# A graph network's first stage: x times the first weights per node, gathered as 96-float rows

## The reference

```
h = concat([x[src], edge_attr])          # 32 + 16 columns
h = relu(h @ w1a + b1a)                  # 96 columns
h = h @ w1b + b1b
s = segment_sum(h, dst); agg = s / max(count(dst), 1)
```

## Time and profile before

| what | us |
|---|---|
| median of 3 runs | 15099.62 (15078.14 to 15099.76) |
| span of the profiled execution | 18914.5 |
| `prepare`, to the next block's first instructions | 0 to 282 |
| quarters 0 and 1, no groups | 282 to 380 |
| first stage, groups | 380 to 7697 |
| node network | 7697 to 7892 |
| propagation | 7892 to 12603 |
| tensor messages | 12603 to 18914.5 |

### The profile page before, as it was taken

How to read it: one execution, slowest core, us unless ns; L and a number is a source line. 1 busy time by engine, 2 the same in 40 slices (tenths; PEclk the granted TensorE clock), 3 DMA queues, 4 the chain that set the end, 5 groups by cost and what they waited for, 6 DMA issues and landing times. The chain is left out here.

```text
span 18914.5 us, 402579 instructions
## 1 busy us (share of the span) xinstructions
PE 14494.5 (77%) x139778; PEld 9671.3 (51%) x139779; DVE 10873.1 (57%) x15415; ACT 5258.0 (28%) x10677; POOL 7506.3 (40%) x8530
## 2 busy tenths in 40 slices
PE   2666666666666666799999999977787778777877
PEld 2555555555555555655555555544444444444444
DVE  6444444444444444455555555557787777777777
ACT  2333333333333333100000000014444444444443
POOL 4444444444444444000000000026676666666765
PEclk8666666666666666699999999989999999999999
DMA  2100010101010010165666566541111111111111
GB/s 72 23 21 22 21 22 20 23 20 23 21 23 21 21 23 21 60 190 187 190 188 190 188 191 190 171 122 27 27 28 28 28 27 28 28 27 27 28 27 27
DMA packets 1143323, 1240.77 MB, mean 66 GB/s; under 512 B 399134, under 2 KB 1111834, under 8 KB 1142394
## 3 DMA queue, kind: packets, MB, share of 16 engines
q1 hardware_dynamic: 932485, 1124.29, 19.8%
q0 software_dynamic: 210496, 113.01, 4.2%
HBM read 1143.04 MB, written 93.60 MB: 65 GB/s over the span
## 5 line engine op out<-in xcount | busy, mean ns | idle before, releaser
L1500 POOL DMA_INDIRECT m_src<-x_after_layer,m_idx x3240 | 3130.8, 966 | 6032.8 <-DMA m_idx<-in_src 4921.4
L180 POOL DMA_INDIRECT l_xin<-in_x,l_idx x3240 | 3095.0, 955 | 4382.1 <-DMA l_idx<-in_src 3211.4
L1232 PE MATMUL p_prod<-a_slot,f_parts 128*32 128x448 fp8e4 x90552 | 4318.4, 353 | 105.4 <-DVEq L1397 50.6
L1232 PEld LDWEIGHTS p_prod<-a_slot,f_parts 128*32 128x32 bf16 x90552 | 2428.9, 97 | 1932.8 <-issue 115.6
L1631 PE MATMUL radial_ps<-radial_w,radial_hidden 128*128 128x384 f32 x6480 | 2598.2, 538 | 719.1 <-DVE m_products L1770 420.0
L581 PE MATMUL a_ps<-hot_hi,hot_lo 128*128 128x196 bf16 x6272 | 1640.4, 303 | 1902.7 <-ACT a_image L680 958.9
L749 DVE TENSOR_TENSOR hot_hi<-window_hi,number_ps 128x1568 bf16<-128x1568 f32 x784 | 1401.2, 1787 | 2895.4 <-PE degree_ps L582 1502.9
L1636 PE MATMUL m_visit_ps<-m_products,m_onehot 128*128 128x288 f32 x8420 | 2445.4, 440 | 561.8 <-DVE m_onehot L1737 261.8
L1636 PEld LDWEIGHTS m_visit_ps<-m_products,m_onehot 128*128 128x128 f32 x8420 | 1669.8, 201 | 1370.3 <-issue 767.9
L1631 PEld LDWEIGHTS radial_ps<-radial_w,radial_hidden 128*128 128x128 f32 x6480 | 1212.8, 202 | 1992.9 <-issue 793.3
L680 ACT ACTIVATE a_image<-a_ps 128x392 fp8e4<-128x392 f32 x3136 | 1478.5, 496 | 2644.6 <-PE a_ps L581 1672.3
(11 more groups left out here) (203 smaller groups left out, 12640.4 us busy)
## 6 DMA issues: line engine op xcount, KB each, us to landing
a_nibbles<-multiplicity_digit SPq DMA_DIRECT2D x1085, 784.0 KB, 4.4
edge_w<-in_edge_weight SPq DMA_DIRECT2D x324, 320.0 KB
multiplicity_digit<-a_packed SPq DMA_DIRECT2D x392, 196.0 KB
l_xin<-in_x,l_idx POOLq DMA_INDIRECT x3240
m_src<-x_after_layer,m_idx POOLq DMA_INDIRECT x3240
xt<-in_edge_attr SPq DMA_DIRECT2D x324, 80.0 KB, 2.2
edge_directions<-rel_unit SPq DMA_DIRECT2D x12, 675.0 KB
m_unit<-edge_directions SPq DMA_DIRECT2D x324, 25.0 KB
```

What stands on the lines that cost most here:

```text
L180: pool.indirect_dma_start(k.xin[m][:, j, :], None, k.io["x"], bass.IndirectOffsetOnAxis(k.idx[m][:, j:j + 1], 0)).then_inc(k.gathered[m], 16)
L1232: mm = nc.tensor.matmul(view(prod[rows, w, :], 0, [[QW, 2], [1, QW]]), source[:, h * HH + j, r * D:(r + 1) * D], slots[h][:, 2 * w:2 * w + ...
L1500: pool.indirect_dma_start(src[m][:, j, :], None, k.x3_d, bass.IndirectOffsetOnAxis(idx[m][:, j:j + 1], 0)).then_inc(gathered[m], 16)
```

## The change

In `prepare`, PE transposes x in 25 quads of four node blocks, multiplies each by a block-diagonal copy of the first 32 rows of `w1a` and adds the bias by a second product (`first_products`); ACT copies the result and stores it to DRAM as `xw_d`, 96 floats a node (`copy_products`). x is loaded at the start. Of the six early gathers one stands between the two rounds of window rows and five behind the second.

In the first stage the gathers fetch 96-float rows of `xw_d`. The attributes are laid out on 80 partitions. Each of a group's two hidden steps is one product of the attributes with a block-diagonal `w1e` and one product of the identity with the gathered rows, both 480 columns wide, summed in PSUM. The transposes and the copies to `xt` are gone. The products of the first visit stand two at a time between single count pairs (`BETWEEN_STEPS`); DVE writes the first one-hot behind a group's first batch, further visits behind its last.

```diff
 def gather_group(k, pool, m):
     for j in range(G):
-        pool.indirect_dma_start(k.xin[m][:, j, :], None, k.io["x"],
+        pool.indirect_dma_start(k.xin[m][:, j, :], None, k.xw_d,
...
-    RC = 270
+    RC = 216
...
+            sp.dma_start(k.x[:], io["x"].rearrange("(b p) f -> p b f", p=P)).then_inc(x_loaded, 16)
+            sp.dma_start(b_quad[:], ...).then_inc(x_loaded, 16)
+            sp.wait_ge(fine_ready, 1)
+            for j in range(4):
+                sp.dma_start(w_quad[j * D:(j + 1) * D, j * DH:(j + 1) * DH], io["L0_gnn_w1a"][0:D, :]).then_inc(x_loaded, 16)
...
+            def copy_products(t):
+                m = t % STAGES
+                if t >= STAGES:
+                    act.wait_ge(first_stored[m], t // STAGES * 16)
+                for j in quads(t):
+                    n = in_quad(j)
+                    act.wait_ge(first_ready, j + 1)
+                    nc.scalar.copy(view(k.xin[m][:], j % 2 * (4 * DH), [[1, n * DH]]), turn_ps[:, 2 + j % 2, 0:n * DH]).then_inc(first_copied, 1)
+                first, end = 8 * t, min(8 * t + 8, NB)
+                act.wait_ge(first_copied, quads(t).stop)
+                act.dma_start(k.xw_d[first * P:end * P, :].rearrange("(b p) c -> p b c", p=P),
+                              k.xin[m][:, 0:end - first, :]).then_inc(first_stored[m], 16)
...
+            def first_products(t):
+                for j in quads(t):
+                    n = in_quad(j)
+                    pe.wait_ge(x_turned_copied, t + 1)
+                    if j >= 2:
+                        pe.wait_ge(first_copied, j - 1)
+                    to = turn_ps[:, 2 + j % 2, 0:n * DH]
+                    nc.tensor.matmul(to, x_turned[0:n * D, t % 2, j % 2 * P:(j % 2 + 1) * P], w_quad[0:n * D, 0:n * DH], start=True, stop=False)
+                    nc.tensor.matmul(to, ones[:], b_quad[0:1, 0:n * DH], start=False, stop=True).then_inc(first_ready, 1)
...
-STEPS_PAIRS = ((4, 4, 4), (4, 2, 2))
+BETWEEN_STEPS = {3: (2, 2, 2, 1, 1, 1, 1, 2), 2: (1, 1, 2, 1, 0, 1, 0, 2)}
...
             def hidden(g, m, b):
-                pe.wait_ge(xt_evac, g + 2)
                 pe.wait_ge(h_evac, g * 2 + (b + 1))
-                for t in range(HT):
-                    mm = nc.tensor.matmul(h_ps[:, t * DH:(t + 1) * DH], xt[:, m % 2, (b * HT + t) * EP:(b * HT + t + 1) * EP], w1a[:],
-                                          start=True, stop=True)
-                mm.then_inc(h_ready, 1)
+                to = h_ps[:, b, 0:HT * DH]
+                nc.tensor.matmul(to, attr[:, m % 2, b * EP:(b + 1) * EP], w1e[:], start=True, stop=False)
+                nc.tensor.matmul(to, k.ident[:], view(xin[m][:], b * (HT * DH), [[1, HT * DH]]), start=False, stop=True).then_inc(h_ready, 1)
...
-            def visits(g, twos, n):
+            def visits(g, twos, n, between):
...
+                one_hot(onehot[n], first).then_inc(onehot_ready, 1)
+                add(dve.snap(count, min_val=0, max_val=NG * NB))
...
+                between()
+                with dve.If(end - first > 1):
```

More of the change, by code:

```diff
@@ L229, in prepare @@
     ident_ready = sem("ident_ready")
+    x_turned_ready, x_turned_copied = sem("x_turned_ready"), sem("x_turned_copied")
+    first_ready, first_copied = sem("node_first_ready"), sem("node_first_copied")
+    STAGES = 2
+    first_stored = [sem(f"node_first_stored{m}") for m in range(STAGES)]
+    quads = lambda t: range(2 * t, min(2 * t + 2, QUADS))
+    in_quad = lambda j: min(4, NB - 4 * j)
+    TURNS = -(-QUADS // 2)
     rel_loaded = [sem(f"rel_loaded{n}") for n in range(2)]
@@ L297, in _ @@
                                         bass.IndirectOffsetOnAxis(at[0][:, g:g + 1], 0)).then_inc(fine_rows, 16)
-            early(2)
+            for m in range(STAGES):
+                await_alone(pool, k.passed_pool, first_stored[m], len(range(m, TURNS, STAGES)) * 16)
+            early(0)
             await_alone(pool, k.passed_pool, key_stored, 32)
@@ L303, in _ @@
                                         bass.IndirectOffsetOnAxis(at[1][:, g:g + 1], 0)).then_inc(key_rows[g // WD], 16)
-            for m in range(3, NX):
+            for m in range(1, NX):
                 early(m)
@@ new lines, in hidden, with product @@
+                nc.tensor.matmul(to, attr[:, m % 2, b * EP:(b + 1) * EP], w1e[:], start=True, stop=False)
+                nc.tensor.matmul(to, k.ident[:], view(xin[m][:], b * (HT * DH), [[1, HT * DH]]), start=False, stop=True).then_inc(h_ready, 1)
+            def product(m, one, tiles):
+                for j in tiles:
+                    mm = nc.tensor.matmul(visit_ps[:, 0:P], hid[m % 2][:, j, :], onehot[one][:, j, :],
+                                          start=(j == 0), stop=(j == G - 1))
+                if G - 1 in tiles:
@@ L624, in visits @@
                     mm.then_inc(product_done, 1)
                     pe.reg_add(count, count, 1)
-            def group(g, twos, m, turn, q, at):
[L629 to L633, removed]
-                first, end = blocks(pe, g)
-                pairs(q, at, run[0])
-                at += run[0]
-                hidden(g, m, 1)
-                pairs(q, at, run[1])
-                at += run[1]
-                if m < NX - 1:
-                    transposes(g + 1, m + 1, turn)
-                visits(g, m, first, end)
-                pairs(q, at, run[2])
-                return at + run[2]
@@ L646, in _, with further_visits @@
-            pe.wait_ge(weights_loaded, 32)
+            def further_visits(m, first, end):
+                with pe.If(end - first > 1):
+                    with pe.Fori(first + 1, end):
+                        v = pe.snap(count, min_val=0, max_val=NG * NB)
+                        pe.wait_ge(onehot_ready, v + 1)
+                        await_alone(pe, k.passed_pe, added, v + 2)
+                        product(m, 2, range(G))
+            def group(g, twos, m, turn, q, at):
+                runs = BETWEEN_STEPS[BATCHES[m]]
+                first, end = blocks(pe, g)
+                for step, count_pairs in enumerate(runs):
+                    pairs(q, at, count_pairs)
+                    at += count_pairs
+                    if step == 0:
+                        pe.wait_ge(loaded[m % 2], twos * 32 + 32)
+                        pe.wait_ge(gathered[m], turn * (16 * G) + 16 * G)
+                    if step < 2:
+                        hidden(g, m, step)
+                    elif step < 7:
+                        tiles = range((step - 2) * 2, (step - 1) * 2)
+                        if step == 2:
+                            v = pe.snap(count, min_val=0, max_val=NG * NB)
+                            await_alone(pe, k.passed_pe, h_evac, g * 2 + 3)
+                            await_alone(pe, k.passed_pe, onehot_ready, v + 1)
+                            await_alone(pe, k.passed_pe, added, v + 2)
+                        if step == 4:
+                            await_alone(pe, k.passed_pe, h_evac, g * 2 + 4)
+                        product(m, m % 2, tiles)
+                further_visits(m, first, end)
+                return at
@@ L647, in _ @@
+            pe.wait_ge(weights_loaded, 16 * HT)
             pe.wait_ge(zero_ready, 1)
```

142 lines of the change are left out of this document (73 added, 69 removed).

## The result

The changed kernel takes 15156.02 us (median of 4 runs, 15137.57 to 15180.15), the kernel before 15097.29 (15078.14 to 15099.76): a ratio of 1.0045, 95% interval 1.003 to 1.0059, so 45 to 89 us more. Forecast were 15,131 and 31 us more.

What follows compares the result with a forecast made beforehand. The prediction took POOL's ten gathers a group to bound the first stage. Wider gathers, PE's work and the shorter chain counted 0, prepare +31 us: 15099.6 + 31 = 15,131, range 14,860 to 15,320.

Steps and rivals of the forecast that it cites:

- The reading of the first stage: First stage: POOL's ten gathers a group set its pace, to within 283 us.
- The late signals: First stage, profiled: PE's signals arrive after POOL's gathers have ended; the profile's own, 3814.9 us over the unprofiled time.
- the floor of 3930 and the cap of 4213: First stage, unprofiled: at least POOL's gathers plus issue time, 3930 us; at most what other stages leave, 4213 us.
- the shorter chain from gather to relu: First stage, transposes and copies gone: taken as 0, lower end -283 us, since SP loads indices six groups ahead.
- its 283 us: First stage: the gap between its least and greatest unprofiled length, where any waits at handoffs had to be.
- point 3 of prepare: Prepare: ACT's 13 turns end at 90 us (half clock 118), seven direction pieces at 126, under 132.
- the half-clock end (+53): Prepare: upper end of its growth, +53 us, if PE's products ran at half clock and direction pieces ended at 154.
- The other terms of prepare: Prepare: window numbers some 8 us later, second round 147.5 to 213.2, 50 gathers 62.6 us, POOL through at 275.8.
- The first rival: First stage waited at handoffs, not at POOL's pace: up to 283 us gained, 14,848 with prepare; chance 0.36.
- My sum of PE's records: First stage: PE gets 0.45 us a group more at full clock, up to 1.35; costed at nothing beside POOL.
- The second rival: First stage bound by PE at a mean clock of 0.757: 190 us slower, 15,320 with prepare; chance 0.12.
- The third: Prepare: its growth is hidden because the window-part chain ends it at 275 in either kernel, about 15,100; chance 0.10.

Runs made afterwards that it cites:

- The first experiment: On the changed kernel, seven of ACT's square roots stand between the node products' turns instead of behind all 13: 15129.92 us, ratio 1.0034.

## Why the prediction was right in direction, and 28 us short

**The reading of the first stage held.** The late signals were the profile's own, and the old stage, seen without them, is at POOL's pace: 4114 us, between the floor of 3930 and the cap of 4213. Two terms made the floor 184 too low, some 90 us each. The mean gather of the earlier trace rows is 952 ns, and without late signals it is 980, because in the old trace only 9 gathers of the loop were held up by a packing, not 54. The issue time of 872.6 us is 962.4 there, because in the old trace some 300 gathers (an estimate: 90 us at 0.30 each) stood behind a wait instead. The ten gathers a group are still there, at the same price for wider rows, so the stage is as long as before (4121 against 4114).

**Luck has a part in that.** The prediction put the shorter chain from gather to relu at nothing, because SP loads indices six groups ahead. What the runs show is a near tie: with half of the gathers the old stage still takes 4100 us, 14 less than with all. Had the other engines needed some 100 us more, the same edit would by these rows have shortened the stage, and the prediction could not tell: it had only its 283 us.

**The step that failed is point 3 of prepare**, the end of ACT's turns. I took 90 us (118 at half clock) and saw the direction pieces covered by the first round of window rows. Each product of 384 columns takes 1.64 us for its two records (0.79 from start to start), where the sum had 0.355 a record from the earlier trace rows. ACT's turns end at 123.8, the seventh piece at 162, and the second round starts at 177.58 instead of 147.5. The first experiment gives that back in the trace (27.4 us). So the first end of the sum was right in its mechanism, "to 154, and then 22 us are late", and the choice was wrong: I took the messages' full-clock row, and PE ran the node products at the half clock. Their records have the durations of that level (ns min/median/max; the products, then records of 384 columns in the messages from 9504.7 to 9509.7 us at a granted clock of 0.50, and from 9548.9 to 9551.0 at 1.00):

```profile
L460 PE MATMUL turn_ps<-w1a_quad,x_turned x50: 524/847/1009, 42.5 to 121.9; 128*128 128x384 f32 x48, 64*128 64x192 f32 x2
```
```profile
L1691 PE MATMUL radial_ps<-radial_w,radial_hidden x8: 804/847/1009, 9504.8 to 9509.4; 128*128 128x384 f32 x8
```
```profile
L1691 PE MATMUL radial_ps<-radial_w,radial_hidden x4: 486/486/590, 9549.2 to 9550.3; 128*128 128x384 f32 x4
```

The 1.00 in the row for 41 to 124 is no reading: the trace's first record of the clock lies at 331.6 us, and the row for 0 to 20, where PE ran nothing, says 1.00 as well.

```profile
0.00:20.00 20.00, 0.00 (x0) 0.01 (x1) 0.90 (x6) 1.30 (x2) 0.76 (x7) 1.00 0.92 186
```

Even the half-clock end (+53) fell short of the 65.5 of POOL's end, in the main since the products began at 41 instead of 36 and the second round took 68.5 us instead of 65.7.

**The other terms of prepare held.** The first window numbers moved 8.7 us (67.64 against the earlier trace rows; 8 in the sum). The 50 gathers took 64 us (62.6 in the sum). The barrier follows POOL's end in both kernels, 9.3 us behind in the one and 7.7 in the other. 438.3 - 374.8 = 63.5 us of later start and 7 us of longer stage are 70, beside the 59 (45 to 89) measured.

**The first rival** (faster by handoffs) was right that the transposes and copies made a longer chain, and wrong that anything waited for it: the change shortens the other engines' part by 4100 - 3776 = 324 us, and POOL hides it. My sum of PE's records pointed the other way, 0.45 us a group more. PE's hidden records did grow (in the old stage and the new, grouped rows of the loop's time):

```profile
L612 PE MATMUL h_ps<-w1a,xt 49*128 49x96 f32 x6430 | 956.5, 298 | 178.7 <-ACT xt L688 178.7
L604 PE MATMUL xt_ps<-ident,l_xin 128*128 128x128 f32 (+1 forms) x963 | 169.5, 288 | 1.4 <-DMA l_xin<-in_x,l_idx 1.4
```
```profile
L661 PE MATMUL h_ps<-w1e_tiles,e_attr 80*128 80x480 f32 x1288 | 763.2, 678 | 160.9 <-DMA l_xin<-x_first_weights,l_idx 160.3 <-issue 0.2
L662 PE MATMUL h_ps<-l_xin,ident 128*128 128x480 f32 x1288 | 717.7, 642 | 0.0
```

from 1126 to 1481 us, and the waits for ACT's copies (178.7) went. So the sum of PE's busy time was not what set the pace of the old stage's other engines. Which of the edits gives the 324 us (no transposes, no copies, or the products spread between the pairs) stays open: they were not tried apart.

**The second rival** (PE the bound) fell: the clock is 0.93 in the stage, PE is busy 86% of it, and POOL waits 0.6 us for it. The prediction's argument that a PE busy all the time would be at full clock is not borne out where this kernel could show it: from 41 to 124 us PE was busy 82.34 of 83 us, with records at half-clock durations to the end. **The third** (prepare's growth hidden by the window parts) fell too: those end at 219.6, not at 275.

## What to carry to other kernels

When a stage runs at the pace of one engine's instruction issue, count first what a change does to that engine's start and to its number of instructions. What it saves on the others is worth nothing until that engine is relieved: with half of the gathers the changed kernel gained 345 us and the old one 19. Work that is added to a preparation on an engine with time to spare must still not stand in that engine's queue ahead of an instruction that others wait for: ACT's 13 turns ahead of a 0.4 us square root delayed POOL's loop by 27 us. Where a row's granted clock has no record behind it, as here in prepare, the durations of the records show the level. A profile whose span is far off the unprofiled time can also hide things, here most of the gathers held up by DVE.

## What the runs showed of the hardware

An indirect gather that POOL issues while DVE runs one of two instructions with both inputs in SBUF ends only behind it: it takes 2.6 to 3.8 us instead of 0.94 over the 3.0 us packing, and the longest gather of the earlier trace rows, 6345 ns, lies over the 6.69 us sum of the earlier trace rows. Cut into seven pieces of 0.56 us, the same packing costs POOL about 26 us over the stage instead of 125 (sum of what gathers take beyond 946 ns).

PE busy 82.34 of 83 us, from 41 to 124, did not bring the clock up, by the durations: its records of 384 fp32 columns kept the 847 ns median that they have at a granted clock of 0.50 (486 at 1.00). Why it stayed down is open. Such a record took 0.79 us from start to start there and 0.32 to 0.43 at 1.00.
